# Four merged stages and a mixture of experts on one core: other orders at the seams, centring of weights later, one row buffer per routing group, slot filling ahead of the barrier, x asked for first

## What is computed

```python
x = x + _L0_xattn_ref(_layernorm(x, axis=-1), ctx_1024, fside, fside, Wq, Wkv, Wout, bout)   # 32 heads of 8, rotary
x = x + _L0_ffn_ref(_layernorm(x, axis=-1), w_r, b_r, w1, b1, w2, b2)      # the best half of a batch's rows, gelu
x = x + _L1_xattn_ref(_layernorm(x, axis=-1), ctx_1024, ...)               # 16 heads of 16, q and k normalised by head
x = x + _L1_ffn_ref(_layernorm(x, axis=-1), gate_w, wg, wu, wd)            # 64 experts, 8 per row, 64 rows per expert
...
logits = x @ gate_w.T
probs = jax.nn.softmax(logits.astype(jnp.float32), axis=-1)
w, sel = jax.lax.top_k(probs, K)
pos = jnp.sum(jnp.cumsum(oh, axis=0) * oh, axis=-1) - 1
valid = pos < CAP
h = jax.nn.silu(jnp.einsum('ech,ehi->eci', inp, wg)) * jnp.einsum('ech,ehi->eci', inp, wu)
```

## Time and profile before

| | |
|---|---|
| median of 3 runs | 1088.85 us (1087.84 to 1093.96) |
| profiled execution, its own time | 1086.34 us |
| its span, first to last instruction | 1084.6 us |
| busy share of the span | TensorE 81%, VectorE 61%, ScalarE 39%, GpSimd 31% |
| mean granted TensorE clock | 0.905 of full speed |
| moved by DMA | 64.78 MB, mean 60 GB/s |

### The profile page before, as it was taken

One profiled execution on the slowest core, in us unless ns is written; L12 is line 12 of the kernel. 1 busy time (PEld: TensorE's weight loads), 2 busy tenths in 40 slices (PEclk: granted clock), 3 DMA queues, 4 the chain that ended last, 5 costly groups with the idle time before them and its releaser, 6 DMA issues. The chain is left out here.

```text
span 1084.6 us, 25643 instructions
## 1 busy us (share of the span) xinstructions
PE 876.2 (81%) x9176; PEld 679.1 (63%) x9176; DVE 664.8 (61%) x1469; ACT 425.4 (39%) x1011; POOL 338.6 (31%) x297
## 2 busy tenths in 40 slices
PE   0699999999998899999789999999996750287740
PEld 0377777777776698898567777777775640154420
DVE  5477777777778255555367777777763449554420
ACT  1144443444343233334255555555655530032210
POOL 0343433434344020000133333333331010367860
PEclk9799999999999599999899999999998655598985
DMA  9200000000005000000001111111110684197547
GB/s 296 63 16 16 13 12 15 15 15 10 15 15 175 1 11 1 0 0 0 3 16 26 29 29 29 31 30 34 29 30 15 204 287 144 44 261 158 96 59 150
DMA packets 79560, 64.78 MB, mean 60 GB/s; under 512 B 41120, under 2 KB 74144, under 8 KB 79008
## 3 DMA queue, kind: packets, MB, share of 16 engines
q1 hardware_dynamic: 72800, 50.62, 16.1%
q0 software_dynamic: 6720, 13.64, 6.8%
HBM read 45.97 MB, written 22.45 MB: 63 GB/s over the span
## 5 line engine op out<-in xcount | busy, mean ns | idle before, releaser
L403 ACT ACTIVATE pr_t<-bank 128x512 f32<-128x512 f32 x128 | 76.4, 597 | 165.3 <-PE bank L299 164.5
L824 POOL TENSOR_TENSOR g_k_bd<-g_k_t,head_mask 128x1024 f32<-128x1024 f32 x32 | 60.6, 1893 | 132.3 <-ACT g_k_t L1001 132.3
L311 PEld LDWEIGHTS bank<-v_bd,pr_t 128*64 128x64 f32 x2048 | 73.1, 142 | 28.2 <-issue 27.9
L299 PE MATMUL bank<-ident,sub 128*128 128x128 f32 x512 | 85.5, 291 | 5.6 <-ACT pr_t L403 5.1
L311 PE MATMUL bank<-v_bd,pr_t 128*64 128x18 f32 x2048 | 86.0, 217 | 0.1
L819 POOL TENSOR_TENSOR xres<-xres,g_out_bias 128x256 f32 (+1 forms) x32 | 23.3, 729 | 178.6 <-DVE g_xn L1026 178.6
L299 PEld LDWEIGHTS bank<-ident,sub 128*128 128x128 f32 x512 | 58.0, 145 | 33.0 <-issue 17.4
L480 DVE TENSOR_TENSOR sub<-bank,top 128x2048 f32<-128x2048 f32 x32 | 73.3, 2292 | 3.9 <-DVE top L476 0.2
L476 DVE TENSOR_REDUCE top<-bank 128x32 f32<-128x2048 f32 x32 | 73.1, 2284 | 0.5 <-PE bank L287 0.4
L260 POOL TENSOR_TENSOR rot<-part_a,part_b 128x512 f32<-128x512 f32 x32 | 40.7, 1273 | 103.9 <-DVE part_b L489 103.9
L643 ACT ACTIVATE f_hid<-bank,b 128x128 f32<-128x128 f32 x128 | 36.5, 368 | 88.7 <-PE bank L589 88.6
(11 more groups left out here) (196 smaller groups left out, 2069.2 us busy)
## 6 DMA issues: line engine op xcount, KB each, us to landing
e_w_gu<-in_experts_in SPq DMA_DIRECT2D x16, 768.0 KB, 6.0
e_w_d<-in_experts_out SPq DMA_DIRECT2D x16, 384.0 KB, 7.6
table<-r_row SPq DMA_DIRECT2D x16, 320.0 KB, 3.2
xres<-in_x SPq DMA_DIRECT2D x4, 1024.0 KB, 9.4
extra<-zero SPq DMA_DIRECT2D x8, 512.0 KB, 5.9
out<-xres SPq DMA_DIRECT2D x32, 128.0 KB, 1.7
out<-extra POOLq DMA_DIRECT2D x4, 1024.0 KB, 14.3
keys_in<-in_ctx_t SPq DMA_DIRECT2D x32, 64.0 KB, 1.8
```

The lines of the kernel that those rows point to most:

```text
L299: m = pe.transpose(b_pr[:, j * P:(j + 1) * P], sub[:, v, cols], k.ident[:, :])
L311: m = pe.matmul(b_o[64 * b:64 * b + 64, hp * VW0:(hp + 1) * VW0], pr_t[:, e, j, b * S:(b + 1) * S], v_bd[:, v, b, hp, :], start=True, stop ...
L403: act.activation(pr_t[:, e, :, :].rearrange("p j q -> p (j q)"), b_pr[:, :], ACT.Exp).then_inc(a_exp, 1)
L824: pool.tensor_tensor(k_bd[:, v, :, :, :, :].rearrange("p c b h s -> p (c b) h s"), k_t[:, v, :, :].rearrange("p c (b a s) -> p (c b) a s", ...
```

## The change

The arithmetic is the same. What differs:

1. All four quarters of x are asked for right behind the constants, ahead of the weights; the statistics of x are written out without a loop.
2. GpSimd does the small addition `g_vb_col` first and then waits until the first pair of feed-forward results has been added (`f_x2` of 2) before it centres the weights.
3. At the seam from a to f, TensorE runs the last output product of a before the picking products of f's first pair. The product of the value bias stands there too, and no longer at the seam from f to g.
4. At the seam from f to g, g's first normalisation and head variances come ahead of the feed-forward additions (`g_head`, `g_rest`); the first square of ScalarE is ahead of the gelus; the late statistics are read by ScalarE a step later.
5. At the seam from g to r, the early statistics (26 tiles, were 28) are taken a step earlier and the first group's rows are normalised before the next probabilities.
6. `r_row` has a buffer for each of the 8 groups, and the waits for stored rows are gone; the ring of expert weights has 9 buffers instead of 10.
7. `fill_slots` stands ahead of the barrier, behind routing.

The semaphores of the row statistics are shared (`k.summed` and others), which changes no wait's meaning.

```diff
-RING_E = 10
+RING_E = 9
-EARLY_F, EARLY_G, EARLY_R = 28, 26, 28
-ROWS_R = 4
+EARLY_F, EARLY_G, EARLY_R = 28, 26, 26
...
-            load_x(0)
+            for c in range(PARTS):
+                load_x(c)
             for dst, src in weights:
                 sp.dma_start(dst, src).then_inc(a_weights, 16)
             both(0, 0, 0)
             both(1, 0, 1)
-            for c in range(1, PARTS):
-                load_x(c)
...
-                with dve.Fori(c * NT // PARTS, (c + 1) * NT // PARTS) as t:
+                for t in range(c * NT // PARTS, (c + 1) * NT // PARTS):
                     dve.bn_stats(tile_of(k.raw, t), tile_of(k.xres, t)).then_inc(a_raw, 1)
...
             pool.wait_ge(k.loaded, 16 * len(k.later_loads))
+            pool.tensor_tensor(k.vb_col[:, :], k.vb_cols[:, 0:KC], k.vb_cols[:, KC:2 * KC], ALU.add).then_inc(k.g_vbcol, 1)
+            pool.wait_ge(f_x2, 2)
             heads = k.wcen[:, :].rearrange("p (h d) -> p h d", d=HD1)
...
-                if g >= ROWS_R:
-                    act.wait_ge(row_out[g % ROWS_R], 32 * (g // ROWS_R))
...
         def _(pe):
-            f_step = f.tensor(pe)
-            turn(f_step, NQ, 4, 0)
             turn(a_step, NT, 5, NT + 2)
-            turn(f_step, NQ, 4, 1)
+            f_step, f_rows = f.tensor(pe)
+            f_rows(0, 0)
             turn(a_step, NT, 5, NT + 3)
+            f_step(1, 0, 1, [True, True, False, False], ranked=True)
+            pe.wait_ge(k.g_vbcol, 1)
+            pe.wait_ge(k.a_x1, NT)
+            for c in range(KC):
+                m = pe.matmul(bank(0)[:, 0:D], k.vb_col[:, c:c + 1].to_broadcast([P, P]), k.wo1[:, c, :],
+                              start=(c == 0), stop=(c == KC - 1))
+            m.then_inc(k.g_vbo, 1)
...
+            s.tensor(pe)
...
         def _(act):
             turn(g_step, NT, 5, 0)
+            g_square(0, 0)
             turn(f_step, NQ, 4, NQ + 1)
             act.preload_act_table_set("natural_log_exp_and_others")
-            turn(g_step, NT, 5, 1)
-            row_scales(act, k, k.g_stats, k.g_rowln, k.g_rowrstd, last_g, 1)
-            turns(act, g_step, NT, 5, 2)
+            g_step(1, 0, 1, [True, True, False, False, False], squared=True)
+            turn(g_step, NT, 5, 2)
+            row_scales(act, k, LATE_G_SUMS, last_g)
+            turns(act, g_step, NT, 5, 3)
+            row_scales(act, k, EARLY_R_SUMS, first_r)
             turn(g_step, NT, 5, NT)
-            row_scales(act, k, k.r_stats, k.r_rowln, k.r_rowrstd, first_r)
+            r_step, r_normalise = r.scalar(act)
+            r_normalise(0)
             turn(g_step, NT, 5, NT + 1)
-            r_step = r.scalar(act)
+            turn(g_step, NT, 5, NT + 2)
             r_step(0)
-            turn(g_step, NT, 5, NT + 2)
             r_step(1)
...
         def _(dve):
+            dve.wait_ge(k.g_vbo, 1)
+            dve.tensor_tensor(k.out_bias[:, :], bank(0)[:, 0:D], k.bo1[:, :], ALU.add).then_inc(k.g_obias, 1)
             turn(f_step, NQ, 4, 2)
...
-            turn(f_step, NQ, 4, NQ)
+            f_step(NQ, NQ // 2, 0, [False, True, False, True])
...
+            turn(g_head, NT, 5, 0)
+            f_step(NQ, NQ // 2, 0, [False, False, True, False])
+            turn(g_rest, NT, 5, 0)
+            f_step(NQ + 1, NQ // 2, 1, [False, False, False, True])
+            turn(g_head, NT, 5, 1)
+            f_step(NQ + 1, NQ // 2, 1, [False, False, True, False])
+            turn(g_rest, NT, 5, 1)
...
+            s.vector(dve)
         inner.close()
-        nc.clear_and_free_semaphores([n for stage in (a, f, g, r) for n in stage.signals])
+        nc.clear_and_free_semaphores([n for stage in (early, a, f, g, r, s) for n in stage.signals])
         nc.all_engine_barrier()
```

More of the change, by code:

```diff
@@ L113, in row_scales @@
[L113 to L123 removed]
+                             op0=ALU.mult, op1=ALU.add).then_inc(k.summed, 1)
@@ L126, in row_shifts @@
-    dve.wait_ge(shift_done, ahead + 1)
+                             op0=ALU.mult, op1=ALU.mult).then_inc(k.shifted, 1)
+    dve.wait_ge(k.shifted, ahead + 1)
 class Shared:
@@ L571, in tensor, with rank_rows, step @@
             pe.wait_ge(k.loaded, 16 * len(k.later_loads))
-            def step(n, i, u, on):
+            def rank_rows(q, v):
+                pe.wait_ge(f_score_done, 2 * q + 2)
+                if later(q, 1):
+                    pe.wait_ge(f_tied_done, 2 * q)
+                for j in range(2):
+                    mm = pe.transpose(b_row[:, j * P:(j + 1) * P], score[:, v, j:j + 1].to_broadcast([P, P]), k.ident[:, :])
+                mm.then_inc(f_row, 1)
+            def step(n, i, u, on, ranked=False):
                 q, m, f = n - 1, n - 2, n - 3
                 v = 1 - u
-                if on[1]:
-                    pe.wait_ge(f_score_done, 2 * q + 2)
-                    if later(q, 1):
-                        pe.wait_ge(f_tied_done, 2 * q)
-                    for j in range(2):
-                        mm = pe.transpose(b_row[:, j * P:(j + 1) * P], score[:, v, j:j + 1].to_broadcast([P, P]), k.ident[:, :])
-                    mm.then_inc(f_row, 1)
+                if on[1] and not ranked:
+                    rank_rows(q, v)
                 def up(half):
@@ L628, in step @@
                     mm.then_inc(f_y, 1)
-            return step
+            return step, rank_rows
         def scalar(act):
@@ L838, in tensor @@
         def tensor(pe):
-            pe.wait_ge(g_vbcol, 1)
-            pe.wait_ge(k.f_pickTc, NQ)
             pe.wait_ge(k.f_xsTc, NQ)
             pe.wait_ge(k.f_centred, 1)
-            for c in range(KC):
-                m = pe.matmul(b_v[:, 0:D], vb_col[:, c:c + 1].to_broadcast([P, P]), k.wo1[:, c, :], start=(c == 0), stop=(c == KC - 1))
-            m.then_inc(g_vbo, 1)
             def scores_ready(a):
@@ L955, in scalar, with square, step @@
             act.wait_ge(g_fill, 4 + 8)
-            def step(n, i, u, on):
+            def square(tk, v):
+                act.wait_ge(g_qk_s, tk + 1)
+                if later(tk, 2):
+                    act.wait_ge(g_var_s, tk - 1)
+                act.activation(sq[:, v, :], qk[:, v, :], ACT.Square).then_inc(g_sq_s, 1)
+            def step(n, i, u, on, squared=False):
                 t, tk, a, w, f = n, n - 1, n - 2, n - 3, n - 4
@@ L965, in exps @@
                     act.activation(pr_t[:, e, :, :].rearrange("p j q -> p (j q)"), b_pr[:, :], ACT.Exp).then_inc(g_exp, 1)
-                if on[1]:
-                    act.wait_ge(g_qk_s, tk + 1)
-                    if later(tk, 2):
-                        act.wait_ge(g_var_s, tk - 1)
-                    act.activation(sq[:, v, :], qk[:, v, :], ACT.Square).then_inc(g_sq_s, 1)
+                if on[1] and not squared:
+                    square(tk, v)
                 if on[3]:
@@ L1012, in step, with head @@
                                        b_v[rows, :].rearrange("p (e m d) -> p e m d", e=2, d=HD1), ACT.Copy).then_inc(g_vc, 1)
-            return step
+            return step, square
         def vector(dve):
-            dve.wait_ge(g_vbo, 1)
             dve.wait_ge(k.f_centred, 1)
-            dve.tensor_tensor(out_bias[:, :], b_v[:, 0:D], k.bo1[:, :], ALU.add).then_inc(g_obias, 1)
-            def step(n, i, u, on):
-                t, tk, a, w, f = n, n - 1, n - 2, n - 3, n - 4
+            def head(n, i, u, on):
+                t, tk = n, n - 1
                 v = 1 - u
@@ L1072, in step @@
                     dve.tensor_tensor(qk[:, u, :], b_qk[:, :], k.wcen[:, 4 * D:6 * D], ALU.add).then_inc(g_qk_s, 1)
-            return step
+            def step(n, i, u, on):
+                head(n, i, u, on)
+                rest(n, i, u, on)
+            return step, head, rest
         return Stage(z.signals, sync=sync, gpsimd=gpsimd, tensor=tensor, scalar=scalar, vector=vector)
@@ L1184, in step @@
                 g = n
-                if not g:
-                    normalise(0)
                 if g < groups:
@@ L1589, in _ @@
             r.sync(sp)
+            s.sync(sp)
         @block.gpsimd
@@ L1750, in _ @@
         def _(dve):
-            s.vector(dve)
             x.vector(dve)
         inner.close()
-        nc.clear_and_free_semaphores([n for stage in (own, ring, s, x) for n in stage.signals])
+        nc.clear_and_free_semaphores([n for stage in (own, ring, x) for n in stage.signals])
         nc.all_engine_barrier()
```

186 lines of the change are left out of this document (89 added, 97 removed).

## The result

The changed kernel takes 1037.6 us (median of 4 runs, 1036.89 to 1038.37) against 1088.34: a ratio of 0.953, 95% interval 0.9498 to 0.9562. That is 50.7 us less; I had said 41 (1048 us). The profiled execution took 1038.37 us, its span is 1036.6 us, 48.0 under the span of before. One execution of the study, of the run with eight row buffers, was a slow one, 1462.18 us at a mean granted clock of 0.56, and its ratio leaves it out.

A forecast was written before the change was run, and what follows sets the result against it. TensorE bounds the first attention and the feed-forward loop, left unchanged; the change works between them. Seven terms sum to 41.7 off 1086.3, giving 1044.6; 2.5 for the median gives 1047.1, said as 1048 us; range 1034 to 1065.

The forecast's parts named there:

- 1, the start: Start of the kernel: x asked for first and statistics written out, so VectorE waits less; 6.8 us off.
- 2, the seam from a to f: First attention to feed-forward: centring later and last tile first; 13.8 us off if the clock holds, 3.5 if not.
- the clock holds: Forecast case: the clock does not fall at the seam from a to f; 1037 to 1057 us, chance 0.55.
- five terms: Seam a to f: TensorE's stop 2.5, drain piece at full clock 3.9, next step 4.5, tail 1.7, first w1 products 1.2.
- I take 0: Feed-forward loop: centring moved there costs nothing; up to 2.8 us lost if an addition falls on the ranking.
- the rival: Feed-forward: VectorE and GpSimd block each other, 2.8 more; experts lose the whole load, 1.8 more; 1050 to 1060, chance 0.05.
- 3, from f to g: Seam f to g: value bias product, idle time and low-clock products go; 5.3 us off, 3.4 if the clock falls.
- 4, from g to r: Seam g to r: TensorE's waits of 2.15 and 2.27 us are undone; 4.4 us off, bounds 2 to 6.
- 5, routing: Routing stage: waits for stored rows go; 9 us off, between about 5 at low clock and 13 at high.
- the high case (13): Routing: if the clock stays high, the stage takes about 29 us, 13 off.
- 6, the filling: Between routing and slot filling: VectorE's idle 6.18 us goes, the 1.8 us barrier is paid once behind filling; 4.4 us off.
- 7, the ring: Experts' stage: with 9 buffers one load of four experts' weights moves into its first steps; 2 us on, nothing to 3.8.

The follow-up runs named there:

- the run with six pieces: The kernel before, with GpSimd's 128 x 1536 centring addition written as six of 128 x 256 in the same place: 1088.97 us, ratio 0.9994.

## Why the prediction held, step by step

- **1, the start**, 6.8 against 7.9. Right in its mechanism. The first quarter came at 8.41, not 8.95, and a quarter takes VectorE 2.71 us, not 2.95. TensorE's first work comes 2.3 us behind the statistics in both traces, not 1.8, so it moved with them and the weights cost nothing.
- **2, the seam from a to f**, 13.8 against 14.5, of which the loop gives 0.66 back. This was the likeliest case of the rivals: the clock holds. Its five terms, 2.5, 3.9, 4.5, 1.7 and 1.2, measured 2.6, 3.9, 4.1, 2.6 and 1.4; the tail was the one taken too small. The run with centring later alone and the one with it early again put 11.7 and 12.3 us on the addition. "I take 0" for the centring in the loop was nearly right and for a wrong reason: the rival had the addition meet the scores, but it met instructions with an operand in PSUM, and the loss came from clearings, which I had not counted. The rule of the Trainium skill that I weighed (page "SBUF — State Buffer", section "Who interferes with whom") also says that `tensor_scalar` can run in a form that needs the shared ports, which whoever issues first then holds for a whole instruction, and that an instruction with at most one SBUF input does not contend otherwise. The rows of `f_pick` (3.19 us) and `f_ys` (0.42) agree, and so does the run with six pieces for instructions with two SBUF inputs. That `f_pick` runs in that form no row shows, and it waited for four clearings in a row, not for one instruction.
- **3, from f to g**, 5.3 against 5.4 in the two profiled executions (4.7 and the 0.66), by partly other terms. The product and the idle 0.90 went as said. The step "I let them and the four query products before them run at the high one: 1.9" failed in this execution: the key products took 1.91 as before. Of the seven traces with the new order here, four have these products at full clock (1.03) and three at half for all or part, so the step was a matter of chance. (The row has four key products, not the 16 that I wrote.) In its place the later waits for `g_xn` and `g_hat`, 0.84, 1.50 and 1.82, became 0, 0.90 and 0.93. Against the other traces of the old order the seam is worth about 7. That 5.3 met 5.4 is luck: other terms made up for the one that failed.
- **4, from g to r**, 4.4 against 4.6, and 4.4 by the run with the old order.
- **5, routing**, 9 against 12.6. The step that was mis-sized is "I take 9, between them": the clock rose again in the second slow group, so the high case (13) was the one to take. My own evidence against it, that it never rose again in the trace before, misread that trace: the gate products took 2.79 us at 841.66 and 1.90 at 845.62, and the clock was down for good only behind the stop of 4.80, while each group brought another wait for stored rows (2.5 to 3.8 us on ScalarE). Even with four buffers it rose behind that stop in two other traces, for one or two groups each time (centring later alone at 850 and 863, statistics written out at 857), each time behind a shorter wait (1.1 to 1.8). With eight buffers and the ring of 9, and no other edit, it rises in the second slow group and stays up.
- **6, the filling**, 4.4 against 4.3, with the price that depends on 5, as the run with the filling behind the barrier shows.
- **7, the ring**, 2 against 0.7, and that is no price: over all traces the experts' stage takes 147.6 to 152.3 us with 10 buffers (five traces, mean 150.0) and 148.3 to 152.3 with 9 (nine, mean 150.1).

Of the 6.3 us by which the sum fell short (41.7 against 48.0) 3.6 are routing, 1.1 the start and 1.3 the experts' stage. Of the 2.7 between 48.0 and 50.7, 2.0 are what the profiled execution of the kernel before lay under its median. It had no second low stretch at the seam from f to g (2 us), and its experts' stage was 2.5 under the mean; which of the two it was is not shown. Why the experts' stage varies by 4.7 us was not tried. One sum of the prediction does not come out: the parts that it names as outside the range are 0.11 (half of 0.14, and 0.04), not 0.17.

## What to carry to other kernels

Read a stop of TensorE together with the granted clock behind it: here a stop that was 2.6 us too long cost 12, and the cure was to move one block of GpSimd's work; reordering TensorE alone gave 1.6. Before pricing the removal of a wait, look at who else stands in the same queue: the stores freed by more buffers piled up in front of the barrier, so the filling ahead of the barrier, 4.3 us by the rows beside the slow routing, is worth 8.6 beside the fast one. Price a stretch from more than one execution where it can go at either clock.

## What I had not expected of the hardware

- GpSimd's four clearings in a row (0.53, 0.53, 0.10 and 1.91 us) held up a `tensor_scalar` pair of VectorE's, 3.19 us for 0.54, though they read nothing; with the last one moved the pair took 1.35. VectorE did not slip in between the clearings as it did between the six additions, and no run tells why. The addition of 2.81 us just before did not lengthen a VectorE addition that reads PSUM (0.42).
- The clock at 1.2 or 2.4 GHz is not settled by the program alone. After the same stops (0.95 and 1.08 or 1.09 us) it held in one execution and fell in the other; at the seam from f to g the changed kernel's two traces have it at half for 4 us and not at all. In g's drain the changed kernel holds it through 0.72 and 1.02 us, and the run with the centring early again loses it after 0.71 and 1.02, which makes its stretch 31.0 us instead of 29.5. It fell at once or within 2 us after each of the stops of 2.15 to 3.82 us read above, and held through the 1.20 in a.
- An issue of two stores of 320 KB takes SyncE 0.9 to 1.0 us in the kernel before, where they land in 3.2 us by the median, and up to 3.70 in the changed kernel (3.93 with the filling behind the barrier), where they land in 8.4.
